# Handing out the first reads of the partial sums block by block, and putting the first expert pair's output ahead of the second pair's work

## What is computed

```
idx, w  = router(x)                       # 6 of 64 experts per token
shared  = relu2(x @ su.T) @ sd.T
xd      = tokens gathered by expert       # 64 experts x 64 slots x 256
h       = relu2(xd @ w1[e].T)             # 128 hidden values
yd      = h @ w2[e].T                     # 256 values per slot
routed  = scatter-add of gate * yd back to the tokens
out     = x + shared + routed
```

## Time and profile before

| what | before |
|---|---|
| median of 3 runs | 1298.58 us (1298.52 to 1301.24) |
| time of the profiled execution | 1299.52 us |
| span in its trace | 1297.7 us |
| granted TensorE clock, mean | 0.969 |
| PE, DVE, ACT, POOL busy over the span | 87%, 68%, 51%, 43% |
| first add issued by POOL | 1193.37 us |
| last add issued, landed | 1263.59 us, 1267.43 us |
| last sum ends on DVE | 1295.27 us |

### The profile page before, as it was taken

One profiled execution on the slowest core, in us unless ns is written; L12 is line 12 of the kernel. 1 busy time (PEld: TensorE's weight loads), 2 busy tenths in 40 slices (PEclk: granted clock), 3 DMA queues, 4 the chain that ended last, 5 costly groups with the idle time before them and its releaser, 6 DMA issues.

```text
span 1297.7 us, 24599 instructions
## 1 busy us (share of the span) xinstructions
PE 1131.1 (87%) x8487; PEld 723.2 (56%) x8487; DVE 885.7 (68%) x1850; ACT 657.6 (51%) x1575; POOL 556.6 (43%) x725
## 2 busy tenths in 40 slices
PE   5799989989999988999999988989999889889930
PEld 3355567665555566665555566655555666654510
DVE  3677886656877875657878865658777766662427
ACT  4655524667455525667555346666555246522630
POOL 1255571210477841210776922202777612144760
PEclk9899999999999999999999999999999999889975
DMA  8465643300343323101533333002433536076889
GB/s 339 151 212 178 191 137 94 82 3 26 102 149 130 109 66 99 33 7 42 161 119 109 100 78 99 2 22 82 131 120 106 189 114 208 2 252 201 156 193 327
DMA packets 120138, 159.57 MB, mean 123 GB/s; under 512 B 11632, under 2 KB 82928, under 8 KB 119280
## 3 DMA queue, kind: packets, MB, share of 16 engines
q1 hardware_dynamic: 106384, 131.73, 32.7%
q0 software_dynamic: 9216, 19.98, 5.9%
q10 hardware_dynamic: 4416, 6.29, 1.3%
HBM read 104.55 MB, written 40.83 MB: 112 GB/s over the span
## 4 chain that ended last, share of the span: by engine, by line
PE 47%; DVE 19%; ACT 11%; issue 9%; POOL 8%; DMA 5%; SPq 0%; POOLq 0%; DVEq 0%; ACTq 0%
PE bank L1197 11%; DVE pool_c L1713 6%; PE bank L1239 5%; PE bank L1116 4%; ACT joint L854 3%; PE bank L1429 3%; PE bank L1386 3%; PE bank L1414 3%; POOL joint L2229 2%; PE bank L1233 2%; ACT pool_c L815 2%; PE bank L1349 2%; PE bank L1218 2%; DMA acc<-pool_b,target 2%; PE bank L1516 2%
## 5 line engine op out<-in xcount | busy, mean ns | idle before, releaser
L1197 PE MATMUL bank<-xm,joint 128*128 128x512 f32 x544 | 268.1, 617 | 18.8 <-DVE pool_c L1713 12.9
L2229 POOL TENSOR_TENSOR joint<-joint 128x512 f32<-128x512 f32 x128 | 164.1, 1283 | 200.7 <-DVE joint L1729 197.7
L1713 DVE SCALAR_TENSOR_TENSOR pool_c<-bank,params,pool_c 128x511 f32<-128x511 f32 (+2 forms) x216 | 161.6, 748 | 87.2 <-ACT pool_c L815 81.3
L1197 PEld LDWEIGHTS bank<-xm,joint 128*128 128x128 f32 x544 | 98.7, 195 | 122.3 <-issue 93.2
L1914 DVE TENSOR_REDUCE nmax<-bank 128x1 f32<-128x384 f32 (+3 forms) x176 | 109.7, 638 | 61.7 <-PE bank L1387 60.9
L1239 PE MATMUL bank<-wout,pool_c 128*128 128x256 f32 x512 | 121.8, 381 | 3.4 <-DVE pool_c L1754 3.4
L854 ACT ACTIVATE joint<-bank,dt_ 128x64 f32<-128x64 f32 x512 | 112.1, 343 | 22.9 <-PE bank L1116 22.5
L1239 PEld LDWEIGHTS bank<-wout,pool_c 128*128 128x128 f32 x512 | 95.7, 190 | 36.1 <-issue 21.7
L2223 POOL DMA_INDIRECT xslot<-xrow,slots x96 | 96.0, 1000 | 25.8 <-issue 22.1
L824 ACT ACTIVATE pool_c<-pool_c 128x512 f32<-128x512 f32 x64 | 40.3, 629 | 115.8 <-DVE pool_c L1713 115.8
L982 ACT ACTIVATE pool_c<-bank 128x512 f32<-128x512 f32 (+1 forms) x156 | 83.3, 551 | 18.2 <-PE bank L1416 16.2
(11 more groups left out here) (276 smaller groups left out, 2382.4 us busy)
## 6 DMA issues: line engine op xcount, KB each, us to landing
pool_b<-dA_rows SPq DMA_DIRECT2D x64, 256.0 KB, 3.4
pool_b<-dec_rows SPq DMA_DIRECT2D x96, 128.0 KB, 3.7
joint<-pool_b SPq DMA_DIRECT2D x96, 128.0 KB, 2.4
acc<-xrow SPq DMA_DIRECT2D x13, 640.0 KB, 6.7
joint<-dA_rows SPq DMA_DIRECT2D x32, 256.0 KB
dA_late<-dA_rows SPq DMA_DIRECT2D x32, 256.0 KB
joint<-acc SPq DMA_DIRECT2D x32, 256.0 KB, 7.0
xslot<-xrow SPq DMA_DIRECT2D x16, 321.0 KB, 5.2
```

Of the source, the lines that this page charges most:

```text
L1197: last = mm(bank[:, :], win[:, k, col:col + P], xm[:, k, :], start=(k == 0), stop=(k == KD - 1))
L1713: ins = v.scalar_tensor_tensor(out=cv[:, n:L], in0=bank[:, 0:L - n], scalar=convw[:, ci, TAPS - 1 - n:TAPS - n], in1=cv[:, n:L], op0=ALU.m ...
L2229: M_ready.inc(p.tensor_tensor(M[u % 2][:, hs_, :], Lx[:, hs_, :], cbm[:, c * P:(c + 1) * P].unsqueeze(1).to_broadcast([P, 4, P]), ALU.mult))
```

## The change

SP's reads of copies 0 and 1 are no longer issued together when set 0 has ended. Block 0 is read then; blocks 1, 2 and 3 are each read when add 25, 27 and 29 has landed; blocks 4 to 7 are read after sets 1 and 2 have ended, ahead of copies 2 and 3. In the expert loop's opening, pair 0's turned hidden values come ahead of pair 1's hidden products on PE, and pair 0's output comes right behind those, ahead of the turns of pair 3, the hidden products of pair 2 and the turned hidden values of pair 1. ACT scales pair 0's output ahead of squaring pair 1, and DVE computes pair 0's targets ahead of clipping pair 1. Nothing is added to or removed from the arithmetic.

```diff
             wait_set(sp, 0)
-            for g in range(BLOCKS):
+            load_sums(sp, 0, range(2))
+            for g in range(1, BLOCKS // 2):
+                wait_added(sp, FIRST_SET_ENDS + 2 * g - 2)
                 load_sums(sp, g, range(2))
             for s in range(1, SETS):
                 wait_set(sp, s)
+            for g in range(BLOCKS // 2, BLOCKS):
+                load_sums(sp, g, range(2))
             for g in range(BLOCKS):
                 load_sums(sp, g, range(2, 4))
...
             square(0)
             for i in range(PAIRS):
-                if i + 1 < PAIRS:
+                if 0 < i and i + 1 < PAIRS:
                     square(i + 1)
...
                 ys_ready.inc(ins)
+                if i == 0:
+                    square(1)
...
+            def expert_out(i):
+                pe.wait_ge(hq_ready.sem, hq_ready.upto(i + 1))
+                pe.wait_ge(ys_ready.sem, ys_ready.upto(max(i - 1, 0)))
+                for e in range(2):
+                    last = mm(pb[4 + i % 2][e * CAP:(e + 1) * CAP, 0:D], hq[i % 2][:, e * CAP:(e + 1) * CAP], w2m[i][:, e, :],
+                              start=True, stop=True)
+                y_mm.inc(last)
+
             turn_tokens(0)
             turn_tokens(1)
             hidden(0)
             turn_tokens(2)
+            turn_hidden(0)
             hidden(1)
-            turn_hidden(0)
+            expert_out(0)
             for i in range(PAIRS):
...
                 if i + 1 < PAIRS:
                     turn_hidden(i + 1)
-                pe.wait_ge(hq_ready.sem, hq_ready.upto(i + 1))
...
-                y_mm.inc(last)
+                if i > 0:
+                    expert_out(i)
...
             take_tokens(2)
+            targets(0)
             relu(1)
             for i in range(PAIRS):
...
-                targets(i)
+                if i > 0:
+                    targets(i)
```

## The result

The changed kernel takes 1307.85 us, median of 11 executions, against 1298.89 for the kernel before, also of 11; the ratio is 1.0062 (95% interval 1.005 to 1.0075), some 8 us slower. Two of its executions, of 3790.63 and 2784.2 us, lie far outside the others' 1304.12 to 1312.09 and are not in the ratio; the median of the other nine is 1307.32. The profiled execution took 1306.92 us with a span of 1305.1, 7.4 more than before.

A forecast was written before the change was run, and what follows sets the result against it. The prediction took the last four adds of one set, then DVE alone, to bound the kernel. Late reads +12.3, adds -4.7 and opening -0.1 sum to +7.5 us; put on the median 1298.58, that gives 1306.1 us, range 1301 to 1310.5.

The forecast's parts named there:

- the tail: Stretch from ACT's first read to the end; 30.25 us before, predicted T + 42.5, 12.3 us longer.
- Part 1: Adds 25 to 31: with fewer reads beside them, the last lands 4.7 us earlier, bounds 3.4 and 6.1.
- rival (b): Rival on the last adds: no speedup, since reads hit them in full or set 2's chain waits; 1310.8 us; chance 0.08.
- Part 2: Late reads of set 0 in at T + 13.2, DVE's first sums only then; end 12.3 us longer, bounds 11.4 to 12.8.
- Part 3: Expert loop's opening: add 0 1.5 to 1.9 us earlier, but only 0.1 us of shift stays from add 1 on.
- (a): Rival on the late reads: they don't share with ACT's, in at T + 6.7; 1299.6 us, mostly no change; chance 0.10.
- T: Moment ACT's reads go out, just after the last add lands: 1267.45 us before, predicted 1262.7.
- (c): Rival on the opening: its early start carries through the loop, 1.4 us less, 1304.7 us; chance 0.10.

The follow-up runs named there:

- the split kernel: Changed kernel with DVE's one wait for set 0 split and SP reading block by block behind the adds: 1299.42 us, ratio to before 1.0012.
- the kernel with ACT held: Changed kernel with ACT's 16 reads held until all reads of set 0 are in: 1303.44 us, ratio to before 1.0048.

## Why the prediction was right

1306.1 us was predicted, with 1301 to 1310.5; 1307.85 was measured. The sum of the terms was +7.5, the ratio gives +6.5 to +9.7, and the span grew by 7.4. The mechanism is the one predicted, adds that end earlier and a tail that grows by more, but that the sum and the span agree to 0.1 us is luck: the adds and the tail gave -4.6 and +12.9, which is 8.3 and not 7.6, and the loop's -2.3 us, of which the sum held 0.1, and the +1.4 us of a later opening, which it did not hold, happen to take 0.9 off again.

**Part 1, the adds: right, in size by luck too.** Behind add 25's issue the last add landed 4.6 us earlier (19.5 instead of 24.1), where 4.7 were said, and it does so in other profiles (19.5 to 19.9 in four kernels with these reads, 23.6 to 24.1 in three with the reads as before). Adds 27 and 29 were in flight for 4.75 and 4.13 us, within the 3.8 to 4.9 said; SP's next reads, which wait for their landings, go out at 1251.89 and 1256.88. But two sizes were off and nearly cancel. Undisturbed, the adds would gain 6.4, not 6.1, and the reads that remain cost 1.9, not 1.4, the middle of a range that no row had narrowed. Of these 1.9, 0.56 come by a path that stands only among the conditions of rival (b): by set 1 alone add 31 would have gone out 0.86 us behind the landing of 29, at 1257.72, but POOL was busy with 30, so that it went out at 1258.28. The chain thus runs over set 2: 26 with 5.60 us, 28 with 4.79, then 30, and 31 follows 30 on POOL after 0.30 us of idle. Beside the reads released by a landing on set 1, the add of set 2 already in flight took longer than the add of set 1 issued next (5.60 against 4.75, 4.79 against 4.13; 26 also had block 0's reads beside it).

**Part 2, the late reads: right, a little too small.** 13.9 and 14.1 us in the two kernels, 13.2 said, outside the bound of 13.7. q1 began with 0.58 MB in the first 5.2 us instead of 0.73, and the lag from the bytes to the landing was 1.4 us or so, not 0.9. The prediction's own row gave 1.3 for that lag (0.23 MB at 0.18 MB per us), and it took 0.9 without a reason. The first sums (4.91) and blocks (21.8) are as worked out. That the order of the reads and the one wait make most of the longer tail is shown by the split kernel, which won 7 us; what part of that is the lost cover of the first sums stays open.

**Part 3, the opening: add 0 right, add 1 too small.** At the same clock add 0 comes 1.5 us earlier behind the first token load (10.5 to 9.1), as said. Add 1 gains 0.6 us (12.45 to 11.8, from two profiles with the old order and seven with the new), not 0.1; pair 1's output on PE, which the prediction held still, began 0.3 to 0.5 us earlier too (9.8 us behind the first token load in the two, 9.3 to 9.5 in the seven). By add 26 it is 0.2 us where the clock stayed up (61.8 to 61.6) and 0.8 where it fell (63.5 to 62.7). These are means of profiles that lie up to 1.9 us apart (60.8 to 62.7 in the seven), so no gain is shown there. Most of the profile's 2.3 us (63.7 to 61.4) goes with the clock: with the old order alone the profiles at the two clocks lie 1.7 us apart (63.5 and 61.8).

**The rivals.** (a) did not happen, and could not have won what I gave it: with no other queue moving the late reads took 9.0 us, not T + 6.7. Its price put the rate of both queues, 0.405 MB per us, on one; the earlier trace rows had one queue at 1.45 MB in 5 us, as in the kernel with ACT held. The Trainium skill's page "DMA: Bandwidth & Descriptors", section "Anatomy of one DMA", gives its fit for a single DMA issued by GpSimd; put on these eight reads of SP together it gave 6.8, an estimate, and the 9.0 measured does not agree. (b) did not happen, since the last add landed 4.6 us earlier, though set 2's chain, one of its two reasons, did come to be the path, for 0.56 us. (c) is not seen in the times, but the kernel with the opening alone does not exclude its 1.4 us either.

## What to carry to other kernels

When a transfer is moved out of another's way, look at who waits for it, and whether one wait covers the whole group: here eight reads moved behind the adds took all eight first sums with them, out of the cover in which they had cost nothing. A block read beside the adds cost them 0.5 to 0.8 us (1.9 us for four, 6.4 for eight); read behind them it cost 1.4 us of tail in the best order tried (5.8 for four) and 3.2 in the changed kernel (12.9 for four). So even the best order with four blocks late cost nearly 8 us together, more than the 6.4 of all eight beside the adds. Here, taking the disturbance off a chain would have paid only if the work had found another cover.

## What was not expected of the hardware

An indirect add of 128 rows of 1 KB was in flight for 3.7 to 3.9 us with no reads beside it and up to 7.8 beside plain reads, with 1.56 to 1.61 us of POOL in either case. Eight reads of 256 KB on one queue landed 9.0 us behind the signal that released them with no other queue moving, and 13.9 to 14.1 with a second queue as busy. One queue alone moved 0.30 MB per us, two together 0.40. In the opening the granted clock fell to 0.72 over 6 us in five of the fourteen profiles and stayed at 1.00 in nine, for either order of the work; where it fell, add 1 came 1.2 to 1.7 us later.
